# Gate/up and down products of a SwiGLU feed-forward written as Strassen-type block products

## The reference, cut to what matters

```
mod = (silu(c) @ wmod)                       # c [2, 1024] -> six rows of 1024 for each batch n
sa, ca, ga, sb, cb, gb = mod                 # ga, gb: magnitude at least 0.25
h = layernorm(x) * (1 + ca) + sa             # x [2, 2048, 1024]
# "attention" over the two batch rows, one 2x2 softmax for each of the 1024 features:
x = x + ga * (h + transpose(msg))
h = layernorm(x) * (1 + cb) + sb
y = (silu(h @ W_gate.T) * (h @ W_up.T)) @ W_down.T    # D_FF = 2752, D = 1024
x = x + gb * y
```

## Time and profile before

| | |
|---|---|
| median of 3 runs | 3038.16 us (3037.96 to 3038.5) |
| span of the profiled execution | 3034.9 us |
| TensorE busy | 2995.2 us (99%), granted clock 0.996 of full |
| DVE, ACT, POOL busy | 1439.1, 778.4, 1150.6 us |
| DMA | 350.08 MB, 115 GB/s over the span |

### The profile page before, as it was taken

One profiled execution on the slowest core, in us unless ns is written; L12 is line 12 of the kernel. 1 busy time (PEld: TensorE's weight loads), 2 busy tenths in 40 slices (PEclk: granted clock), 3 DMA queues, 4 the chain that ended last, 5 costly groups with the idle time before them and its releaser, 6 DMA issues.

```text
span 3034.9 us, 36540 instructions
## 1 busy us (share of the span) xinstructions
PE 2995.2 (99%) x13020; PEld 2403.0 (79%) x13020; DVE 1439.1 (47%) x1506; ACT 778.4 (26%) x812; POOL 1150.6 (38%) x964
## 2 busy tenths in 40 slices
PE   8799999999999999999999999999999999999999
PEld 3258888888888888888888888888888888888887
DVE  7985444443444444454444534444444444443333
ACT  4652122222232122221222222322222212222221
POOL 7408242481336540491434722374404914300000
PEclk9899999999999999999999999999999999999999
DMA  8253232422233222422224222332324222232322
GB/s 346 83 195 118 90 111 88 164 87 103 90 124 138 85 104 89 177 92 97 97 98 158 84 103 99 118 136 93 106 78 178 92 94 100 99 126 86 108 86 94
DMA packets 59835, 350.08 MB, mean 115 GB/s; under 512 B 6800, under 2 KB 6800, under 8 KB 33312
## 3 DMA queue, kind: packets, MB, share of 16 engines
q1 hardware_dynamic: 59776, 349.74, 32.4%
q10 hardware_dynamic: 32, 0.03, 0.0%
HBM read 332.93 MB, written 16.81 MB: 115 GB/s over the span
## 4 chain that ended last, share of the span: by engine, by line
PE 95%; POOL 2%; issue 1%; DVE 1%; DMA 1%; ACT 0%; SPq 0%; DVEq 0%; POOLq 0%; ACTq 0%
PE ps L996 21%; PE ps L998 21%; PE ps L997 21%; PE ps L1020 10%; PE ps L1019 10%; PE ps L1021 10%; POOL presum L332 1%; PE ps L894 1%; POOL sq_pair L346 1%; DMA xbuf<-x 1%; DVE dbuf L646 1%; PE ps L929 0%; PE ps L1017 0%; PE ps L1016 0%; DVE xbuf L771 0%
## 5 line engine op out<-in xcount | busy, mean ns | idle before, releaser
L996 PE MATMUL ps<-xn_hi,w_hi 128*128 128x512 f32 x2752 | 1070.9, 389 | 0.0
L998 PE MATMUL ps<-xn_hi,w_lo 128*128 128x512 f32 x2752 | 1070.6, 389 | 0.0
L997 PE MATMUL ps<-xn_lo,w_hi 128*128 128x512 f32 x2752 | 1070.6, 389 | 0.0
L764 DVE TENSOR_TENSOR w_lo<-w_raw,w_hi 128x2048 fp32r<-128x2048 f32 (+2 forms) x304 | 672.7, 2213 | 64.1 <-ACT w_hi L548 63.4
L548 ACT CAST w_hi<-w_raw 128x2048 fp32r<-128x2048 f32 (+2 forms) x304 | 504.9, 1661 | 696.5 <-PE ps L1021 378.3
L996 PEld LDWEIGHTS ps<-xn_hi,w_hi 128*128 128x128 f32 x2752 | 516.7, 188 | 107.4 <-issue 0.4
L997 PEld LDWEIGHTS ps<-xn_lo,w_hi 128*128 128x128 f32 x2752 | 516.7, 188 | 107.2
L998 PEld LDWEIGHTS ps<-xn_hi,w_lo 128*128 128x128 f32 x2752 | 516.7, 188 | 107.0
L829 DVE TENSOR_TENSOR prod<-ps,sg 128x512 f32<-128x512 f32 x168 | 116.1, 691 | 977.2 <-ACT sg L588 977.2
L1020 PE MATMUL ps<-h_lo,w_hi 128*128 128x512 f32 x1344 | 522.9, 389 | 0.0
L1021 PE MATMUL ps<-h_hi,w_lo 128*128 128x512 f32 x1344 | 522.9, 389 | 0.0
(11 more groups left out here) (136 smaller groups left out, 1712.9 us busy)
## 6 DMA issues: line engine op xcount, KB each, us to landing
w_raw<-wgu SPq DMA_DIRECT2D x168, 1024.0 KB, 4.8
w_raw<-wdn SPq DMA_DIRECT2D x128, 704.0 KB, 4.0
wm<-wmod SPq DMA_DIRECT2D x24, 1024.0 KB, 4.9
xbuf<-x SPq DMA_DIRECT2D x8, 2048.0 KB, 12.4
out<-acc SPq DMA_DIRECT2D x64, 256.0 KB, 2.0
x_next<-x SPq DMA_DIRECT2D x7, 2048.0 KB, 7.7
w_raw<-wgut SPq DMA_DIRECT2D x8, 512.0 KB, 3.5
junk_a<-stats SPq DMA_DIRECT2D x7, 512.0 KB, 8.4
```

What stands on the lines that cost most here:

```text
L764: v.tensor_tensor(w_lo[r][:, 0:size], w_raw[r][:, 0:size], w_hi[r][:, 0:size].bitcast(F32), ALU.subtract).then_inc(lo_ready, 1)
L996: mm(banks[j], w_hi[r][:, w], xn_hi[:, k, :], start=k == 0, stop=False)
L997: mm(banks[j], w_hi[r][:, w], xn_lo[:, k, :], start=False, stop=False)
L998: ins = mm(banks[j], w_lo[r][:, w], xn_hi[:, k, :], start=False, stop=k == KD - 1)
```

## The change

The matrix products of the feed-forward are written as 2×2 block products with seven products for eight (Winograd's form of Strassen's rule). For gate and up together, the 2×2 of the weights is (gate, up) × (first, second half of the 1024 features), and the 2×2 of the data is (first, second half of the features) × (chunk a, chunk b). For down it is (even, odd tile of inner features) × (first, second half of the outputs), with the same two chunks. Eight chunks make `NS` = 4 superchunks of two, numbered s (s0 to s3 below).

**Gate/up.** Inner features are 22 tiles (20 of 128, 2 of 96), taken as 11 pairs `g` of two tiles `u`. A pair has 14 products (7 for each tile) in the order `PAIR_ORDER`; product number m of 616 has 4 feature tiles × 3 = 12 matmuls of 512 columns. Products accumulate into banks with earlier ones: P6 and P4 and P7 go on in the bank of P1 after ACT has copied its content out; P3 goes on in the bank of P5. DVE adds and multiplies the results into the four blocks of the inner layer, and then makes three more blocks from sums of them (`t_sums`). All seven blocks are written to DRAM (`h_dram`).

**Weights.** In s0, DVE makes the sums of weight blocks, ACT and DVE split them, and SP stores each split product operand in DRAM (`whl_dram`, two stores of 128 rows of 2 KB for each product). In s1 to s3 SP loads them split, into ten slots, with rows of 4 KB.

**Next norm.** The two chunks of the next superchunk are prepared in four groups (`NGRP`) of 64 positions by 2 batch rows, spread over the products of s0 to s2 by `prep(s, r, o)`, where o is the number of products since `group_base`; one group begins every 33 products. ACT and DVE do what POOL did. x comes in and the seven data blocks go out to DRAM (`xr_dram`) in rows of 64 float32, 256 bytes. At the end of a superchunk the seven blocks are read back whole.

**Down.** After all of gate/up come 28 stages (7 products for each superchunk) of 4 blocks; a block is one weight tile column of 11 × 3 matmuls. The data blocks of a stage come from `h_dram`. In s3 DVE makes the sums of the down weights and SP stores them.

**Start.** ACT and DVE prepare both chunks of s0 before the loop. POOL does nothing after the first part.

The order of the products, the depth of the buffers, and where groups begin:

```diff
+PAIR_ORDER = [("P1", 0), ("P1", 1), ("P5", 0), ("P5", 1), ("P6", 0), ("P6", 1), ("P2", 0),
+              ("P7", 0), ("P2", 1), ("P7", 1), ("P3", 0), ("P4", 0), ("P3", 1), ("P4", 1)]
...
+HI_RING = 7
+SLOTS = 10
+AHEAD = 3
...
+    return M_S * s + (8 if s == 0 else 1) + 33 * r
```

A product on TensorE, with what it waits for:

```diff
+                g, u, name = SEQ[m]
+                s, t, n = g // NPT, 2 * g + u, width(g)
+                if name == "P1" and g:
+                    pe.wait_ge(h1_done, t - 1)
...
+                if name == "P6":
+                    pe.wait_ge(p1_copied, t + 1)
+                if name == "P7":
+                    pe.wait_ge(v_copied, t + 1)
+                if name == "P4":
+                    pe.wait_ge(w_copied, t + 1)
+                if name == "P3":
+                    pe.wait_ge(c22_done, t + 1)
+                if s == 0:
+                    pe.wait_ge(w_ready, m + 1)
...
+                    mm(bank, hi[:, w], x_hi[name][:, k, :], start=fresh and k == 0, stop=False, skip_group_check=not fresh)
+                    mm(bank, hi[:, w], x_lo[name][:, k, :], start=False, stop=False, skip_group_check=not fresh)
+                    ins = mm(bank, lo[:, w], x_hi[name][:, k, :], start=False, stop=k == KH - 1, skip_group_check=not fresh)
+                ins.then_inc(prod_done, 1)
```

SP, for each product of s0, and then its part in a group of the next norm at o = 0 and o = 33:

```diff
+                if s == 0 and p < NPT - 1 and name not in ("P6", "P3"):
+                    sp.wait_ge(prod_done, m + 1)
+                    sp.wait_ge(w_stored[m % HI_RING], 32 * (m // HI_RING + 1))
+                    load_w(2 * (g + 1) + u, (name, u))
+                if EARLY <= m + AHEAD < M_S:
+                    store_w(m + AHEAD)
...
+                if o == 0:
+                    if group == 0:
+                        sp.wait_ge(x_ready, NXF)
+                    else:
+                        sp.wait_ge(xr_stored, 16 * 7 * group)
+                        sp.wait_ge(x2g_stored, 32 * group)
+                    for ab in range(2):
+                        sp.dma_start(xg[:, ab].rearrange("p k n c -> p (k n) c"), x_piece(x[first + ab], r)).then_inc(xg_loaded, 16)
...
+                if o == 33:
+                    sp.wait_ge(tg_ready, group + 1)
+                    for name, of in (("P1", hg[:, 0, 0:KH]), ("P2", hg[:, 0, KH:KD]), ("P5", hg[:, 1, 0:KH]), ("P3", hg[:, 1, KH:KD])):
+                        sp.dma_start(x_piece(xr_dram[s + 1, PRODUCTS.index(name)], r), of.rearrange("p k n c -> p (k n) c")).then_inc(xr_stored, 16)
```

A group's wait for x on DVE, and its small operations on ACT (at o = 3, 5, 7, 9):

```diff
+                if o in (2, 3):
+                    if o == 2:
+                        dve.wait_ge(xg_loaded, 64 * (group + 1))
...
+                    for k in range(KH):
+                        for n in range(NB):
+                            cols = slice(n * PIECE, (n + 1) * PIECE)
+                            s.activation(ub[:, 0, k, cols], hg[:, ab, k0 + k, n, :], ACT.Identity,
+                                         bias=coef[:, 2, n, k0 + k:k0 + k + 1], scale=coef[:, 0, n, k0 + k:k0 + k + 1])
+                            ins = s.mul(ub[:, 1, k, cols], hg[:, ab, k0 + k, 1 - n, :], coef[:, 1, n, k0 + k:k0 + k + 1])
```

A block of the down product on TensorE (its waits left out):

```diff
+                for j in range(NPT):
+                    n = NARROW if j == NPT - 1 else P
...
+                    mm(bank, hi[0:n, w], hh[stage % 2][0:n, j, :], start=fresh and j == 0, stop=False, skip_group_check=not fresh)
+                    mm(bank, hi[0:n, w], hl[stage % 2][0:n, j, :], start=False, stop=False, skip_group_check=not fresh)
+                    ins = mm(bank, lo[0:n, w], hh[stage % 2][0:n, j, :], start=False, stop=j == NPT - 1, skip_group_check=not fresh)
+                ins.then_inc(blk_done, 1)
```

More of the change, by code:

```diff
@@ L31 @@
 KD = D // P
+KH = KD // 2
 CC = 256
@@ L191, in bc @@
+    y_moved, y_done = [sem(f"y_moved{r}") for r in range(Y_RING)], sem("y_done")
     def bc(ap, n):
@@ new lines, in _ @@
+            for e in range(2):
+                load_y(e)
+            for half in range(2):
+                sp.wait_ge(h_stored[half], 16 * NPT * NS)
+            for b in range(NBLK):
+                stage, q = b // NQ, b % NQ
+                if b + 2 < NBLK:
+                    if b + 2 >= 4:
+                        sp.wait_ge(blk_done, b + 2 - 4 + 1)
+                    load_w2(b + 2)
+                if q == 0 and stage + 1 < NSTAGE:
+                    if stage:
+                        sp.wait_ge(blk_done, NQ * stage)
+                    for c in range(len(H_PIECES)):
+                        load_h(stage + 1, c)
+                e = evac_before(b)
+                if evac_before(b + 1) > e:
+                    if e + 2 < NY:
+                        load_y(e + 2)
+                    store_y(e)
@@ L314, in _ @@
+            for r in range(Y_RING):
+                sp.wait_ge(y_moved[r], 32 * len(range(r, NY, Y_RING)))
         @block.gpsimd
@@ new lines, in modulate_f @@
+            def modulate_f(h, k):
+                act.wait_ge(tf_ready, KD * h + k + 1)
+                to = ((raw_b11, raw_b21), (x_raw["P5"], x_raw["P3"]))[h][k // KH]
+                for n in range(NB):
+                    ins = s.activation(to[:, k % KH, n * CC:(n + 1) * CC], xh_f[:, h, k, n, :], ACT.Identity,
+                                       bias=mod[:, 3, n, k:k + 1], scale=cb1[:, n, k:k + 1])
+                ins.then_inc(rawf_ready, 1)
+            w_hi_cast(0)
+            w_hi_cast(1)
@@ new lines, in _ @@
+            for k in range(KH):
+                modulate_f(0, k)
+            for k in range(KH):
+                act.wait_ge(rawf_ready, k + 1)
+                s.copy(x_hi["P1"][:, k, :], raw_b11[:, k, :]).then_inc(xhi_ready, 1)
+            for k in range(KH, KD):
+                modulate_f(0, k)
+            act.wait_ge(x2f_stored, 32)
+            for k in range(KH):
+                act.wait_ge(rawf_ready, KH + k + 1)
+                s.copy(x_hi["P2"][:, k, :], raw_b21[:, k, :]).then_inc(xhi_ready, 1)
@@ new lines, in _ @@
+            invert_f(0)
+            scale_f(0)
+            w_lo_part(0)
+            w_lo_part(1)
+            for k in range(KH):
+                x_lo_f("P1", raw_b11, k)
+            invert_f(1)
+            dve.wait_ge(x2f_stored, 32)
+            for k in range(KH):
+                x_lo_f("P2", raw_b21, k)
+            w_lo_part(2)
+            w_lo_part(3)
+            scale_f(1)
+            dve.wait_ge(rawf_ready, 2 * KD)
+            for u in range(2):
+                dve.wait_ge(mean_saved[u], 16 + 16 * (NPAIR // 2))
@@ L1052, in _ @@
-            with pe.Fori(0, NCH - 1) as e:
-                chunk(e, False)
-            chunk(NCH - 1, True)
+            parts(3, range(GROUP[3]))
+            for h in range(2):
+                for k in range(KD):
+                    pe.wait_ge(x2f_ready, KD * h + k + 1)
+                    ins = mm(ps_mean_f[h], ones[:], tok(x_f[:, h])[:, k, :], start=k == 0, stop=k == KD - 1)
+                ins.then_inc(meanf_mm, 1)
+                turn(2 + h, ps_mod[1 + h], ROWS[2 + h], 0)
+            for h in range(2):
+                for j in range(NSQ):
+                    pe.wait_ge(sqf_ready, NSQ * h + j + 1)
+                    for k in range(SQ_PER):
+                        ins = mm(ps_var_f[h], ones[:], sq_f[:, j % 2, k, :], start=j == k == 0, stop=j == NSQ - 1 and k == SQ_PER - 1)
+                    ins.then_inc(sqf_used, 1)
@@ new lines, in _ @@
+            for m in range(M_ALL):
+                g, u, name = SEQ[m]
+                if g == 0 and name == "P5" and u == 0:
+                    pe.wait_ge(mods_taken, 1)
+                s = g // NPT
+                if s < NS - 1:
+                    for r in range(NGRP):
+                        o = m - group_base(s, r)
+                        if o in (16, 24):
+                            i = (16, 24).index(o)
+                            sum_over_features((ps_mean_g, ps_var_g)[i], NGRP * s + r, i)
+                product(m)
```

1215 lines of the change are left out of this document (762 added, 453 removed).

## The result

The changed kernel takes **3209.39 us** (median of 4 runs, 3206.31 to 3210.47) against 3038.11 of the kernel before on the same chip: a ratio of 1.056 (95% interval 1.0549 to 1.0575). It is 5.6% slower; predicted were 2925 us and, as the upper end, 3035.

What follows compares the result with a forecast made beforehand. TensorE, busy 99% of the span, was taken as the bound. Base 2777 + 48 + 52 + 25 + 15 + 5 = 2922 us of span, with the median 3.3 higher: 2925 us, range 2825 to 3035.

Steps and rivals of the forecast that it cites:

- The base, 2777: Whole kernel if nothing waits: feed-forward in effect from 254, matmuls 2514, statistics 5, tail 4, giving 2777 us.
- ends: Ends of s0, s1 and s2, where data blocks are reloaded: 15 us, then some 5 each, 25 together.
- change to down: Switch from gate/up to down: third weight tile asked for only after the last inner blocks reach DRAM, 5 us.
- I take 31 ns: Next norm's DMA: price of each 256-byte row on an engine, taken from the load of 64-byte rows.
- The ends 8 and 87: Lower and upper limits, in ns, given for the price of one 256-byte row in the next norm's DMA.
- TensorE stands 16 us: s0 group changes: DVE waits 24 us for x, TensorE stands 16 us, for three groups 48 us.
- The rival in which rows of 48 ns or more make the kernel slower: Group changes: dear small rows lengthen waits for stores and x, no gain at 48 ns, about 3300 us at 87; chance 0.11.
- Only P3, which waits for DVE's sum, is held: the slack is 8.2, 27 and 13.6 us: s1 and s2, groups 1, 2 and 3: TensorE stands 16 + 0 + 10 us, twice, 52 us; first groups have no such stores.
- I take 15 us in all (0 to 35): s0 gate/up: ACT runs up to 8 us late with small copies, delaying weight casts; 15 us in all.
- 32 of 38: s0 gate/up: DVE's work, norm included, takes 32 us of the 38 that 14 products last.
- The third rival: s0 runs in step with its DMA queue, late weights delaying sums: 60 to 100 us, 2985 to 3025; chance 0.14.
- The fetch: Loading x and statistics behind seven stores at group changes: TensorE stands 48 us in s0, 52 in s1 and s2.

Runs made afterwards that it cites:

- the run without a norm: Changed kernel with all work on the next stage's norm left out of stages 0 to 2, block inputs read from x instead: 2814.75 us, ratio 0.927.
- the run with long rows: Changed kernel with columns reordered so the norm's x, x2 and block inputs move in rows of 2 or 4 KB, not 256 bytes: 3153.26 us.

## Why the prediction was wrong, step by step

- **The base, 2777, right.** First P1 at 229 and P5 at 269.8 (223 and 265 predicted), TensorE standing 26.4 us before P5; products 2.72 us, s3 420 us, down 850 for 835. Base, ends and change to down came to 2807; the run without a norm has a span of 2810.9. The saved work is there in full.
- **The error, 284 us, in short.** The stands of s1 and s2 take 57 us more than the sum had, the lower clock behind stands and waits 79 where it had nothing, and the short waits of s0 104 (151.1 us between 290 and 880 us, less 47.5 in its three stands) where it had 15 and 15 for the end. The rest is spread over short waits in s1 and s2 (48 us for 10), down (10 us) and smaller ones.
- **"I take 31 ns" for a short row, too dear.** 19 ns when the queue is full. The time from the first of the seven stores to DVE's start on x was 21 us in the stand above; the prediction had 26.4 without the weight stores ahead. The ends 8 and 87 held it. Of the two sections of the Trainium skill's DMA: Bandwidth & Descriptors, Why small descriptors are slow gave some 13 ns by estimate; its 11 cycles for 8 are 38% more time and not 27, so some 15 by estimate, and the trace, with 39% less rate at 256 bytes than at 2 KB, is dearer than either. Specifications, by which short rows are off line rate, agrees with the trace: 214 GB/s for 350. No run here shows whether that is a read-modify-write.
- **"TensorE stands 16 us" in s0, right:** 12.5, 17.5 and 18.7 us from start to start, 49 in all for 48. At the first two the last thing to end before TensorE starts is the weight split, as foreseen, at the third DVE's `hb`. The rival in which rows of 48 ns or more make the kernel slower did not come: the rows are cheap and it is slower all the same.
- **"Only P3, which waits for DVE's sum, is held: the slack is 8.2, 27 and 13.6 us", the first step that failed.** 52 us became 109: the stands of s1 are 10.4, 11.7, 16.3 and 16.6 us, those of s2 9.9, 12.0, 15.3 and 17.1. The stands at P3, groups 1 and 3, are 57 us for 52, though each by itself is off by 4 to 7 us, so that sum is in part luck. The other 52 us are groups 0 and 2, for which I had 0. ACT waits for DVE's `hg` at o = 3, and behind that wait stand the bank copies of P1, P6 and P7, each due two or three products after its own (5.4 or 8.2 us). Group 2 shows it in the lines above. Group 0, without stores ahead, has a stand too.
- **"I take 15 us in all (0 to 35)" for ACT's and DVE's backlog, the step that failed most.** Taking only ACT's small copies away gives back 147 us (134 when GpSimd does them). I had the duration nearly right (4.6 us for sixteen, 5.4 predicted) and counted it against the free time of a weight cast alone. But it holds a queue in which every bank copy stands as well, it comes sixteen times a stage, with sixteen more of half the size, and it lengthens each stand that the fetch makes. DVE's load in s0 ("32 of 38") I worked out and then gave no price; what it costs is not settled: 24 us of s0 come back for 25 us of DVE's time in one run, 9 for 35 in another.
- **The third rival, right in its sign and wrong in its cause.** TensorE's waits stand everywhere in s0, but the DMA share there is 0.68 and not 0.9, and without the stores only 27 us go. What keeps s0 in step is the split of the weights on the two helper engines. Its last sentence, that short waits could lower the clock, was right, and the missing price is 79 us.
- **The fetch** is worth 145 us alone, with the clock that it costs; 100 were predicted, without it. Fetch and ScalarE's copies are shown, each by a run with nothing left out.

## What to carry to other kernels

When work is moved to helper engines that run in order beside a saturated engine, add up not their busy time but how long each of their queues can be held at once, and compare that with the slack of every instruction behind it: here helpers that were 51% and 39% busy let TensorE idle for 335 us in s0 to s2. Follow a wait through all engines: behind DVE's wait for x stood ACT's wait for DVE, and behind that the copy for which TensorE stood. Fetch before storing, move small instructions to an engine on which nothing urgent is queued, give rows their length, and the same arithmetic becomes 4.5% faster than the kernel before. When a list of waits names no cause, look in order of time for what ended just before.

## What the runs showed of the hardware

- After a stand TensorE starts with matmuls 0.43 us apart in place of 0.23, eleven of them where it stood 16 us and nine where it stood 7.3; the granted clock is 0.86 over s0 and 1.00 over s3. In this kernel the cost follows the count of stands more than their length.
- How long SP needs to issue a transfer went with the rows queued ahead of it. The 24 loads of statistics, all of one form, have a median of 2.52 us behind loads of x in 256-byte rows; in the run with long rows it is 0.44, as in

```profile
1112.43 0.38 SPq L414 DMA_DIRECT2D st<-stats  x1
1113.41 0.43 SPq L414 DMA_DIRECT2D st<-stats  x1
```

- A moving operand that is read in four pieces of 128 columns (long rows) costs TensorE nothing: s3 takes 421 us both ways.
- DVE is slower while GpSimd works: its 128x512 low parts of weights have a mean of 0.765 us with GpSimd at work and 0.673 without.
